# A batched 512 x 512 product from split fp32 operands: all transposes on VectorE, the first product copied into the bank of the second, operands made in pairs

## The reference

```python
def reference(x, itok_B_1_98, L0_cond_T):
    Tb = T[fwd_steps - 1]                        # one 512 x 512 matrix for each batch
    x = x + jnp.einsum('bij,bjk->bik', Tb, x)
    return x
# x: 8 x 512 x 512 fp32, T: 100 x 512 x 512 fp32, fwd_steps: 8 indices
```

## Time and profile before

| | us |
|---|---|
| median of 3 runs (lowest to highest) | 116.84 (116.51 to 118.35) |
| span of the profiled execution | 117.3 |
| matmuls of `same` and `diff`, first to last start | 11.46 to 113.7 |
| last sum on VectorE | 114.38 to 114.80 |
| mean granted clock of TensorE, share of full speed | 0.985 |

### The profile page before, as it was taken

The page is one execution under the profiler, slowest core; times in us unless marked ns, Lnnn a source line. Parts: engine busy times, 40 slices in busy tenths (PEclk is TensorE's granted clock), DMA queues, the critical chain, the costliest instruction groups (busy, mean ns, idle before and its releaser), DMA issues. The chain is left out here.

```text
span 117.3 us, 1986 instructions
## 1 busy us (share of the span) xinstructions
PE 108.4 (92%) x512; PEld 89.9 (77%) x512; DVE 96.2 (82%) x139; ACT 67.0 (57%) x125; POOL 81.2 (69%) x68
## 2 busy tenths in 40 slices
PE   4945999999799999999999999999999999999990
PEld 4925888888588877888888888887788878777880
DVE  0196769999946999999978999799989996899681
ACT  2715499658129958458277853995098624933000
POOL 2364587996738957996788876895789586874400
PEclk9996799999999999999999999999999999999999
DMA  2799974448887895447998599749982897222233
GB/s 86 231 310 255 344 205 147 129 105 294 229 296 254 279 320 194 153 124 238 287 257 291 157 293 363 229 122 298 353 242 92 256 278 281 87 89 89 103 133 122
DMA packets 15416, 25.26 MB, mean 215 GB/s; under 512 B 1712, under 2 KB 6064, under 8 KB 15408
## 3 DMA queue, kind: packets, MB, share of 16 engines
q1 hardware_dynamic: 14976, 24.39, 66.6%
q10 hardware_dynamic: 432, 0.79, 2.0%
HBM read 16.78 MB, written 8.39 MB: 215 GB/s over the span
## 5 line engine op out<-in xcount | busy, mean ns | idle before, releaser
L249 POOL TENSOR_TENSOR TD_r<-TH_r,TL 128x512 fp32r<-128x512 f32 x32 | 42.3, 1323 | 21.3 <-DVE TL L290 21.2
L243 POOL TENSOR_TENSOR xL<-x_sb,xH 128x512 fp32r<-128x512 f32 x30 | 39.2, 1308 | 7.1 <-ACT xH L191 7.1
L382 PE MATMUL same<-xH,TH_r 128*128 128x512 f32 x124 | 36.5, 417 | 0.4 <-DVE out_sb L315 0.3
L412 PE MATMUL diff<-xD,TD_r 128*128 128x512 f32 x128 | 34.3, 391 | 0.0
L389 PE MATMUL same<-xL,TL 128*128 128x512 f32 x124 | 33.4, 391 | 0.0
L191 ACT ACTIVATE xH<-x_sb 128x512 fp32r<-128x512 f32 x32 | 20.3, 634 | 22.5 <-DMA x_sb<-x 19.6
L412 PEld LDWEIGHTS diff<-xD,TD_r 128*128 128x128 f32 x128 | 24.0, 188 | 5.0
L389 PEld LDWEIGHTS same<-xL,TL 128*128 128x128 f32 x124 | 23.4, 189 | 5.4
L382 PEld LDWEIGHTS same<-xH,TH_r 128*128 128x128 f32 x124 | 22.0, 195 | 5.2 <-DVE out_sb L315 1.8
L315 DVE SCALAR_TENSOR_TENSOR out_sb<-same,rest 128x512 f32<-128x512 f32 (+1 forms) x33 | 22.3, 676 | 2.9 <-PE same L404 0.2
L290 DVE TENSOR_TENSOR TL<-turned_ps,TH 128x512 fp32r<-128x512 f32 x24 | 16.2, 677 | 8.6 <-ACT TH L199 8.5
(11 more groups left out here) (15 smaller groups left out, 22.6 us busy)
## 6 DMA issues: line engine op xcount, KB each, us to landing
out<-out_sb SPq DMA_DIRECT2D x31, 256.0 KB, 3.8
x_sb<-x SPq DMA_DIRECT2D x29, 256.0 KB, 4.6
T_sb<-T SPq DMA_DIRECT2D x7, 768.0 KB, 5.1
T_cols_sb<-T SPq DMA_DIRECT2D x32, 64.0 KB, 4.1
x_sb<-x ACTq DMA_DIRECT2D x3, 256.0 KB, 3.5
...
out<-out_sb SPq DMA_DIRECT2D x2, 128.0 KB, 1.9
```

The costliest lines, as they stand in the source:

```text
L243: nc.gpsimd.tensor_tensor(xL[s][:, n], x_sb[s][:, n], xH[s][:, n].bitcast(fp32), ALU.subtract).then_inc(done, 1)
L249: nc.gpsimd.tensor_tensor(TD_r[n][:], TH_r[n][:].bitcast(fp32), TL[n][:].bitcast(fp32), ALU.subtract).then_inc(TD_ready, 1)
L382: nc.tensor.matmul(same[n % 2][:], TH_r[n][:, j], xH[s][:, j], start=(j == 0), stop=False)
L412: done = nc.tensor.matmul(diff[n % 2][:], TD_r[n][:, j], xD[s][:, j], start=(j == 0), stop=(j == N - 1))
```

## The change

The whole schedule is written anew, unrolled over 16 pairs of units (k = 0 to 15) in place of a loop.

- **T** comes in 512-byte runs only: four transfers a batch, each of 256 KB into 32 partitions (L108), and for unit 0 of batch 0 four small ones (L115). **VectorE transposes** every tile (32 instructions, L292) from SBUF into a bank of PSUM; it now reads with a step of one element, because the partitions are dealt out as (g u c) instead of (p n). TensorE's 96 transposes go.
- **x and out** are laid out in the same manner, so their transfers, too, are four of 256 KB a batch into (out of) 32 partitions each (L93, L96), and a batch is stored when all its four tiles are summed. x has four slots, its operands three, T two, the operands of T four pairs.
- **The sum**: ScalarE copies -4097 same into the bank of `diff` (L189, "seed"), TensorE adds `diff` onto it without clearing, and VectorE does one subtraction, out = x - diff (L311). `rest` and the second sum go, and so does TH: TL = T - 4096 TH_r (L303).
- **Pairs**: TH_r, TL, TD_r are made for two units in one instruction of 128 x 1024, and xH, xH_copy, xL, xD for two tiles of x (a "half") in one.
- TensorE's order is same(U), diff(U - 1), same(U + 1), and so on. In iteration k, pair k + 2 of T (the tiles two pairs ahead) and half k + 3 of x are made; iteration 0 makes two of each.

The core of the diff:

```diff
-    x_rows = x.rearrange("b (p n) k -> b p n k", n=N)
-    out_rows = out.rearrange("b (p n) k -> b p n k", n=N)
-    T_rows = T.rearrange("t (p n) j -> t p n j", n=N)
-
-    T_cols = T.rearrange("t (m q n) (g c) -> t n g q m c", q=Q, n=N, g=G)
+    WARM = 6
+
+    x_part = x.rearrange("b (g u c) k -> b g c u k", g=G, c=Q)
+    out_part = out.rearrange("b (g u c) k -> b g c u k", g=G, c=Q)
+
+    T_part = T.rearrange("t (m n q) (g c) -> t g q m n c", n=N, q=Q, g=G)
     itok_row = itok.rearrange("(a b) -> a b", a=1)
...
+        def T_pairs(k):
+            return [p for p in ([1, 2] if k == 0 else [k + 2]) if p < PAIRS]
+
+        def x_halves(k):
+            return [h for h in ([2, 3] if k == 0 else [k + 3]) if h < 2 * B]
+
+        def half(tiles, h):
+            return tiles[h // 2 % X_SETS][:, 2 * (h % 2):2 * (h % 2) + 2]
+
+        def load_x(eng, b, g):
+            s = b % X_SLOTS
+            eng.dma_start(x_sb[s][g * Q:(g + 1) * Q], x_part[b, g]).then_inc(x_loaded[s], 16)
+
+        def store(eng, b, g, tiles, done):
+            eng.dma_start(out_part[b, g, :, tiles], out_sb[b % OUT_SLOTS][g * Q:(g + 1) * Q, tiles]).then_inc(done, 16)
...
+            def load_T(t, b, g):
+                sp.dma_start(T_sb[b % T_SLOTS][g * Q:(g + 1) * Q],
+                             T_part[bass.ds(t, 1), g].rearrange("a q m n c -> (a q) m n c")
+                             ).then_inc(T_loaded[b % T_SLOTS], 16)
...
+            for b in range(B):
+                if b + T_SLOTS < B:
+                    t = matrix(b + T_SLOTS)
+                    sp.wait_ge(turned_ready, (b + 1) * N)
+                    for g in range(G):
+                        load_T(t, b + T_SLOTS, g)
+                if b < B - 1:
+                    sp.wait_ge(sum_ready, (b + 1) * N)
+                    for g in range(G):
+                        store(sp, b, g, slice(0, N), stored[b % OUT_SLOTS])
+                    if b + X_SLOTS < B:
+                        for g in range(G):
+                            load_x(sp, b + X_SLOTS, g)
...
+            def cut_x_half(h):
+                b = h // 2
+                act.wait_ge(x_loaded[b % X_SLOTS], 16 * G * (b // X_SLOTS + 1))
+                if b >= X_SETS:
+
+                    act.wait_ge(same_ready, (b - X_SETS + 1) * N)
+                i = 2 * (h % 2)
+                nc.scalar.activation(half(xH, h), x_sb[b % X_SLOTS][:, i:i + 2], COPY, scale=LEAN).then_inc(xH_ready, 2)
+
+            def copy_xH_half(h):
+                act.wait_ge(xH_ready, 2 * h + 2)
+                if h > 2:
+                    act.wait_ge(xD_ready, 2 * h)
+                nc.scalar.activation(xH_copy[:], half(xH, h).bitcast(fp32), COPY).then_inc(xH_copied, 2)
...
+            def cut_T_pair(p):
+                act.wait_ge(turned_ready, 2 * p + 2)
+                if p >= T_SETS:
+                    act.wait_ge(same_ready, 2 * (p - T_SETS) + 2)
+                    act.wait_ge(TD_ready, 2 * (p - T_SETS) + 2)
+                nc.scalar.activation(TH_r[p % T_SETS][:], turned[:], COPY, scale=LEAN / RADIX).then_inc(TH_ready, 2)
+
+            def seed(U):
+
+                act.wait_ge(same_ready, U + 1)
+                if U >= 2:
+                    act.wait_ge(sum_ready, U - 1)
+                nc.scalar.activation(diff[U % 2][:], same[U % 2][:], COPY, scale=-(RADIX + 1.0)).then_inc(seeded, 1)
...
+            for k in range(PAIRS):
+                seed(2 * k)
+                for p in T_pairs(k)[:1]:
+                    cut_T_pair(p)
+                for h in x_halves(k)[:1]:
+                    cut_x_half(h)
+                seed(2 * k + 1)
+                for h in x_halves(k)[:1]:
+                    copy_xH_half(h)
+                for p in T_pairs(k)[1:]:
+                    cut_T_pair(p)
+                for h in x_halves(k)[1:]:
+                    cut_x_half(h)
+                    copy_xH_half(h)
...
+            def cut_x_half(h):
+                b, i = h // 2, 2 * (h % 2)
+                pool.wait_ge(xH_ready, 2 * h + 2)
+                nc.gpsimd.tensor_tensor(half(xL, h), x_sb[b % X_SLOTS][:, i:i + 2], half(xH, h).bitcast(fp32),
+                                        ALU.subtract).then_inc(xL_ready, 2)
...
+            def cut_T_pair(p):
+                s = p % T_SETS
+                pool.wait_ge(TL_ready, 2 * p + 2)
+                if p >= T_SETS:
+                    pool.wait_ge(diff_ready, 2 * (p - T_SETS) + 2)
+                nc.gpsimd.tensor_tensor(TD_r[s][:], TH_r[s][:].bitcast(fp32), TL[s][:].bitcast(fp32), ALU.subtract
+                                        ).then_inc(TD_ready, 2)
...
+            for k in range(PAIRS):
+                for h in x_halves(k)[:1]:
+                    cut_x_half(h)
+                for p in T_pairs(k)[:1]:
+                    cut_T_pair(p)
+                for h in x_halves(k)[1:]:
+                    cut_x_half(h)
+                for p in T_pairs(k)[1:]:
+                    cut_T_pair(p)
...
+            def cut_x_half(h):
+                dve.wait_ge(xL_ready, 2 * h - N + 2)
+                dve.wait_ge(xH_copied, 2 * h - N + 2)
+                if h // 2 >= X_SETS:
+                    dve.wait_ge(diff_ready, (h // 2 - X_SETS + 1) * N)
+                nc.vector.scalar_tensor_tensor(half(xD, h), half(xL, h).bitcast(fp32), -RADIX, xH_copy[:],
+                                               ALU.mult, ALU.add).then_inc(xD_ready, 2)
...
+                    dve.wait_ge(T_loaded[b % T_SLOTS], 16 * G * (b // T_SLOTS + 1))
+                    rows = T_sb[b % T_SLOTS][:, :, n]
+                if U >= 2:
+                    dve.wait_ge(TL_ready, U - 1)
+                nc.vector.transpose(turned[:, U % 2].rearrange("p u (m q) -> p m u q", q=Q),
+                                    rows.rearrange("p m (u c) -> p m u c", c=Q)).then_inc(turned_ready, 1)
...
+            def cut_T_pair(p):
+                s = p % T_SETS
+                dve.wait_ge(TH_ready, 2 * p + 2)
+                nc.vector.scalar_tensor_tensor(TL[s][:], TH_r[s][:].bitcast(fp32), -RADIX, turned[:],
+                                               ALU.mult, ALU.add).then_inc(TL_ready, 2)
+
+            def sum_up(U):
+                b, n = U // N, U % N
+                dve.wait_ge(diff_ready, U + 1)
+                if n == 0 and b >= OUT_SLOTS:
+                    dve.wait_ge(stored[b % OUT_SLOTS], 16 * G * (b // OUT_SLOTS))
+                nc.vector.tensor_tensor(out_sb[b % OUT_SLOTS][:, n], x_sb[b % X_SLOTS][:, n], diff[U % 2][:],
+                                        ALU.subtract).then_inc(sum_ready, 1)
...
+            for k in range(PAIRS):
+                for p in T_pairs(k)[:1]:
+                    turn(2 * p)
+                    turn(2 * p + 1)
+                if k:
+                    sum_up(2 * k - 1)
+                for p in T_pairs(k)[:1]:
+                    cut_T_pair(p)
+                sum_up(2 * k)
+                for h in x_halves(k)[:1]:
+                    cut_x_half(h)
+                for p in T_pairs(k)[1:]:
+                    turn(2 * p)
+                    turn(2 * p + 1)
+                    cut_T_pair(p)
+                for h in x_halves(k)[1:]:
+                    cut_x_half(h)
...
+            def multiply_same(U):
+                b, n = U // N, U % N
+                p, i, s = U // 2 % T_SETS, U % 2, b % X_SETS
+                if U >= 2:
+                    pe.wait_ge(seeded, U - 1)
+                pe.wait_ge(TH_ready, U + 1)
                 for j in range(N):
...
+            def multiply_diff(U):
+                b, n = U // N, U % N
+                p, i, s = U // 2 % T_SETS, U % 2, b % X_SETS
+                pe.wait_ge(seeded, U + 1)
+                pe.wait_ge(TD_ready, U + 1)
                 for j in range(N):
                     if n == 0:
-                        pe.wait_ge(xD_ready, b * N + j + 1)
-                    done = nc.tensor.matmul(diff[n % 2][:], TD_r[n][:, j], xD[s][:, j], start=(j == 0),
-                                            stop=(j == N - 1))
+                        pe.wait_ge(xD_ready, max(2, b * N + j + 1))
+                    done = nc.tensor.matmul(diff[U % 2][:], TD_r[p][:, i, j], xD[s][:, j], start=False,
+                                            stop=(j == N - 1), skip_group_check=True)
                 done.then_inc(diff_ready, 1)
 
-
```

362 lines of the change are left out of this document (112 added, 250 removed).

## The result

| | before | changed |
|---|---|---|
| median of 4 runs each, us (lowest to highest) | 117.59 (116.51 to 120.97) | 154.74 (154.33 to 155.51) |
| ratio to before, 95% interval | 1 | 1.327 (1.319 to 1.334) |
| span of the profiled execution | 117.3 | 153.3 (its time: 155.12) |

The change makes the kernel a third slower: 37 us. The forecast was 149, its range 130 to 158. Some executions of the kernel before (one of the four here) take some per cent longer than the others, and the ratios leave them out; the others took 116.5 to 118.4 us here and, beside the experiments, 117.1 (one run, beside the two single exchanges and both together), 117.2 to 118.7 (three) and 116.8 to 118.1 (five, beside the last two kernels).

A forecast was written before the change was run, and what follows sets the result against it. PE was taken to bound the kernel before; afterwards two circles of waits: start 17.2, rounds 99.8, losses 15.0, end 13.9, last store 3.4, sum 149.3, so 149 us; range 130 to 158.

The forecast's parts named there:

- without a hole on PE: Kernel before: PE's chain runs without a pause, so PE sets the pace, 5.46 us a pair plus 16.1 of transposes.
- The first circle: VectorE transposes, TH_r, xH behind it on ScalarE, xL, xD, next transposes: 7.13 us a round, 14 rounds, 99.8 us.
- The transposes: New VectorE transposes, step one into PSUM: 0.68 us each, not 1.10; two take 1.28 us.
- The second circle: SyncE: T waits behind stores and x loads, which wait for the last sum; 3.75 us lost a batch, 15.0 in all.
- The way: From transposes through last sum, SyncE's issue and 3.15 MB of transfers to T's landing: 18.0 us against two rounds, 14.3.
- Start: Before iteration 0: first loads at about 14.0, then first operands made; iteration 0 starts at 17.2 us.
- two xD 1.3: At the start on VectorE, before iteration 0: two xD operations take 1.3 us together.
- Rounds and losses: Middle of the kernel: 14 rounds, 99.8 us, plus waits for T at batches 3 to 6, 15.0 us.
- The end up to the last sum: From iteration 13's transposes: 3.0 us to diff(27), eleven groups on PE 10.0, last sum 0.84; 13.9 us.
- The last store: Behind the last sum: 3.4 us to the span's end, against 2.5 before, with 768 KB of stores issued just ahead.
- From the span to the median: Sum of 149.3 us, set against the profiled execution, taken as 0.5 above the median of runs: 149 us.
- The clock: PE pauses every round and its granted clock may fall; 1.7 us a round absorbs some, a few us upward.

The follow-up runs named there:

- the two single exchanges: Changed kernel with xH ahead of TH_r on ScalarE: 149.91 us; changed kernel with T ahead of stores and x on SyncE: 139.63 us.
- the last two kernels: Both queue exchanges plus earlier second xH at the start and earlier last stores: 117.10 us; that plus partition-group order 0, 2, 1, 3: 113.52 us.
- the kernel with both exchanges: Changed kernel with xH ahead of TH_r on ScalarE and T ahead of stores and x on SyncE: 119.01 us.
- the transfers alone: Runs of transfers only, without the product: x into 32 partitions 233 GB/s, T into 32 partitions 214, T into 128 partitions 283.
- the third kernel: Changed kernel with xH ahead of TH_r and T ahead of stores and x: 119.01 us.

## Why the prediction was right, and what it missed

**What bounds before.** Not tested by an edit of its own, but the kernel with both exchanges agrees: without transposes on PE, and with no circle, PE is busy without a gap at 5.40 us a pair. The chain that the forecast read as "without a hole on PE" covers only the last 13 us of the kernel before (from 101.98 us on); that PE has no room earlier rests on its waits, 4.3 us in all, and on stretches such as 51 to 65 us, in which it is busy 14.00 of 14.00 us.

**The first circle: right, in its kind and its size.** The round was forecast at 7.13 us and is 7.12. Term by term: transposes 1.31 + 0.09 to TH_r's start (1.28 forecast), TH_r 0.92 to the start of xH (1.00), xH 1.19 to the start of xL (1.10), xL 2.49 to the start of xD (2.45), and 1.12 left for xD up to the next transposes (1.15). Breaking the one link between TH_r and xH took it to PE's 5.40; adding 0.77 us to the transposes took it to 7.87.

**The transposes: right end of the bound taken, for the right reason.** 702 ns with step one, 1086 with step four, into either memory. Here the two rules of the Trainium skill that the forecast weighed, on VectorE's transposing array (Vector Engine (DVE) Microarchitecture Reference, The reshape front-end and per-opcode configuration) and on 16-byte lines (Advanced Engine Details and Errata, SBUF Cachelines), agree with the runs.

**The second circle: right in kind; in size partly because errors cancelled.** The way was put at 18.0 us against two rounds of 7.13, a loss of 3.75 us a batch and 15.0 in all. The four ways measure 17.9, 17.7, 18.8 and 18.3, mean 18.2, and the waits 15.1; moving T ahead gave back 15.1. In the first way the bytes took about 14.0 us (42.5 to 56.5) against 14.5 forecast, and the rest 3.9 against 3.52. But they did not go at 217 GB/s throughout. SyncE's issues in that way:

```profile
44.53 3.14 SPq L93 DMA_DIRECT2D x_sb<-x  x4
50.61 1.93 SPq L108 DMA_DIRECT2D T_sb<-T  x4
```

Stores and x moved at 241 GB/s (42.5 to 50.5), T later at 207 to 220, and between them lies a dip that the forecast didn't have (128 GB/s at a share of 0.58 from 51 to 52): SyncE's last issue of x ends at 47.67 and its first of T comes at 50.61, 2.9 us later. L101, the fetch of T's index in two instructions, stands between them (medians 1.18 and 0.53 us). Most of it is hidden while x is still on the way, the rest leaves the dip; it is also time that an index fetched earlier might give back, which wasn't tried. That the partitions and not the length of the runs set it was the reading that the trace of before couldn't decide; the transfers alone do.

**Where the 5.7 us between 149.0 and 154.7 lie.**
- Start: iteration 0 began at 18.36 instead of 17.2. The step that failed is "two xD 1.3": these first ones read both inputs from SBUF, and two last 2.37 us, the four of them 1502 ns in the mean. The trace of the kernel before had the same form, in a row that I passed over for that of the steady state (group of the kernel before, by line and form):

```profile
L278 DVE SCALAR_TENSOR_TENSOR xD<-xL,xH 128x512 fp32r<-128x512 f32 x4 | 3.5, 917 | 0.0
```

  Even 917 would have given only half of the miss. That GpSimd working beside them is the cause isn't shown by an experiment. In the timeline GpSimd is at work at the same time, and the same operation with one input in PSUM (xH_copy) takes 1222 ns for twice the elements. The trace of before has a clearer row, TL with both inputs in SBUF (duration shortest/median/longest, first and last start):

```profile
L290 DVE TENSOR_TENSOR TL<-turned_sb,TH x8: 680/1280/1350, 18.5 to 108.4; 128x512 fp32r<-128x512 f32 x8
```

  Seven of the eight began while GpSimd's xL was running (as at 57.17, beside the xL of 56.62 in the earlier trace rows), took 1.27 to 1.35 us and ended about 0.55 us after it; the eighth, at 108.37, began 0.09 us before GpSimd's operation ended and took 0.68, and the 24 with one input in PSUM 0.64 to 0.69. The Trainium skill (SBUF — State Buffer, Who interferes with whom) has a rule that fits: an operation of VectorE with two inputs in SBUF and one of GpSimd that reads SBUF block each other. +1.2.
- Rounds and losses: 133.85 - 18.36 = 115.5 against 114.8. +0.7, half of it the one round of 7.42.
- The end up to the last sum: 14.0 against 13.9.
- The last store: 5.4 us against 3.4. The forecast asked how much was issued before, 768 KB, and put a little on top of 2.5; it should have taken those 768 KB and the last 256 at the rate of such transfers: 1.05 MB at the 232 GB/s measured from 148 to 152 us are 4.5 us, from about 147.75 on, and 1 us to land. Storing two of the tiles earlier took the 5.4 to 3.7. +2.0.
- From the span to the median: the forecast set the span of before, 117.3, against the median of the runs and subtracted 0.5. In each run here whose span is known, the time is 1.8 us longer than the span. A span of 117.3 thus belongs to a time of about 119.1, which is none of the runs in the table: the profiled execution of before was a longer one, and not "0.5 above the median". The median lies 1.4 above the profiled span, where the forecast had it 0.3 under its sum. +1.7.

**The clock.** Put down as "a few us on the upper side". It fell as said (0.88 over the profiled execution, 0.50 in the stretch from 20 us), and in the first circle it cost nothing, since PE wasn't in it. It can't be told apart in the tail.

**What was wrong afterwards** was the theory of the third kernel, that 25.5 MB at 213 GB/s are a floor. It took a rate measured while all transfers stand in the same order for a limit of the chip.
